# Second half's cross output projection and norms moved beside the first half's self-attention, second half's self-attention beside the shared expert

## What is computed

```python
# x (8, 100, 512), ctx (8, 361, 256); all float32
x = x + tanh(g_xattn) * xattn(layernorm(x), ctx, Wq, Wk, Wv, Wo)   # 16 heads of 128, 8 key-value heads
x = x + tanh(g_ffn) * ffn(layernorm(x), ...)

def ffn(x, ...):
    h = rms(x, w_ln1)
    q, k, v = h @ wq + bq, h @ wk + bk, h @ wv + bv      # 16 heads of 32
    q, k = rope(q, k)
    ctx = softmax(causal(q k^T / sqrt(32))) @ v
    x = x + ctx @ wo
    h = rms(x, w_ln2)
    probs = softmax(h @ w_router); combine = top 2 of 8 experts
    routed = sum over experts of combine * (silu(h @ w_gate_e) * (h @ w_up_e)) @ w_down_e      # width 352
    sh = (silu(h @ w_sh_gate) * (h @ w_sh_up)) @ w_sh_down * sigmoid(h @ w_sh_eg)              # width 1408
    return x + routed + sh
```

## Time and profile before

| | us |
|---|---|
| median of 3 runs (lowest, highest) | 997.44 (992.25, 1000.63) |
| the profiled execution's own time | 1002.25 |
| its span | 1000.4 |
| busy in the span: TensorE, VectorE, ScalarE, GpSimd | 903.5, 656.2, 565.2, 401.1 |
| mean granted TensorE clock | 0.952 |

### The profile page before, as it was taken

The page is one execution under the profiler, slowest core; times in us unless marked ns, Lnnn a source line. Parts: engine busy times, 40 slices in busy tenths (PEclk is TensorE's granted clock), DMA queues, the critical chain, the costliest instruction groups (busy, mean ns, idle before and its releaser), DMA issues.

```text
span 1000.4 us, 16144 instructions
## 1 busy us (share of the span) xinstructions
PE 903.5 (90%) x5713; PEld 834.9 (83%) x5713; DVE 656.2 (66%) x1492; ACT 565.2 (57%) x1433; POOL 401.1 (40%) x373
## 2 busy tenths in 40 slices
PE   4999999999999999997869787798888989999894
PEld 4889999999989999997848565597888988988894
DVE  4557777743747776722787757586745867888853
ACT  3656666644556666733436657554335767777750
POOL 3432322345532322345645321055371546555531
PEclk9999999999999999998977888799898989999998
DMA  5762000035510000044321111033577799999975
GB/s 140 218 226 84 1 1 1 11 105 146 164 57 16 2 1 1 12 92 118 95 82 44 43 54 33 12 97 104 173 211 213 229 280 271 298 295 288 285 181 144
DMA packets 125689, 120.76 MB, mean 121 GB/s; under 512 B 12645, under 2 KB 96557, under 8 KB 125009
## 3 DMA queue, kind: packets, MB, share of 16 engines
q1 hardware_dynamic: 106510, 96.09, 31.6%
q0 software_dynamic: 5120, 10.22, 5.1%
q10 hardware_dynamic: 13978, 13.41, 4.8%
HBM read 102.16 MB, written 17.53 MB: 120 GB/s over the span
## 4 chain that ended last, share of the span: by engine, by line
PE 54%; DVE 15%; DMA 15%; ACT 6%; issue 5%; POOL 3%; SPq 0%; ACTq 0%; POOLq 0%; DVEq 0%
PE bank L1978 49%; DMA eraw<-in_L_ffn_w_down_e_dram 5%; PE bank L2105 3%; DVE we L1301 3%; DMA s_sum<-yo,target 2%; DMA eraw<-in_L_ffn_w_up_e_dram 2%; ACT we L871 2%; ACT PF L1078 1%; DMA s_rows<-HR,idx 1%; DMA raw<-in_L_ffn_wq_dram 1%; POOL wf L1839 1%; DVE PQ L1485 1%; DMA raw<-in_L_ffn_w_sh_up_dram 1%; DVE sm L1508 1%; DMA sums<-s_sum 1%
## 5 line engine op out<-in xcount | busy, mean ns | idle before, releaser
L1868 POOL TENSOR_SCALAR SC<-SC,mx,anyv 100x361 f32<-100x361 f32 x128 | 81.4, 647 | 210.9 <-DVE mx L1414 200.9
L1839 POOL TENSOR_TENSOR wf<-raw,wf 128x512 fp32r<-128x512 f32 x54 | 74.2, 1382 | 142.9 <-ACT wf L857 142.9
L1851 POOL TENSOR_TENSOR we<-eraw,we 128x704 fp32r<-128x704 f32 x40 | 74.2, 1854 | 108.1 <-ACT we L871 106.6
L1839 POOL TENSOR_TENSOR wx<-raw,wx 128x512 fp32r<-128x512 f32 x64 | 83.1, 1305 | 79.3 <-ACT wx L857 79.2
L871 ACT ACTIVATE we<-eraw 128x704 fp32r<-128x704 f32 (+2 forms) x140 | 96.1, 719 | 32.6 <-DMA eraw<-in_L_ffn_w_down_e_dram 18.2
L1301 DVE TENSOR_TENSOR we<-eraw,we 128x704 fp32r<-128x704 f32 (+2 forms) x100 | 94.9, 967 | 29.2 <-ACT we L871 28.9
L1978 PE MATMUL bank<-H2h,wf 128*128 128x400 f32 x352 | 100.6, 353 | 0.0
L986 ACT ACTIVATE SC<-SC,mx 100x361 f32<-100x361 f32 x128 | 75.4, 593 | 27.9 <-DVE mx L1410 27.2
L857 ACT ACTIVATE wf<-raw 128x512 fp32r<-128x512 f32 x100 | 61.5, 627 | 27.6 <-DMA raw<-in_L_ffn_w_sh_down_dram 9.2
L1978 PE MATMUL bank<-QOh,wx 128*128 128x400 f32 x256 | 72.3, 355 | 5.0 <-POOL wx L1839 5.0
L1978 PE MATMUL bank<-XTh,wx 128*128 128x400 f32 x256 | 72.1, 354 | 3.2 <-POOL wx L1839 1.9
(11 more groups left out here) (265 smaller groups left out, 2790.1 us busy)
## 6 DMA issues: line engine op xcount, KB each, us to landing
eraw<-in_L_ffn_w_gate_e_dram SPq DMA_DIRECT2D x40, 352.0 KB
eraw<-in_L_ffn_w_up_e_dram SPq DMA_DIRECT2D x40, 352.0 KB
eraw<-in_L_ffn_w_down_e_dram SPq DMA_DIRECT2D x40, 256.0 KB
raw<-in_L_xattn_Wq_dram SPq DMA_DIRECT2D x32, 256.0 KB
raw<-in_L_xattn_Wo_dram SPq DMA_DIRECT2D x32, 256.0 KB
raw<-in_L_ffn_w_sh_gate_dram SPq DMA_DIRECT2D x22, 256.0 KB
raw<-in_L_ffn_w_sh_up_dram SPq DMA_DIRECT2D x22, 256.0 KB
s_rows<-Z SPq DMA_DIRECT2D x6, 800.0 KB
```

What stands on the lines that cost most here:

```text
L1839: eng.tensor_tensor(w[:, 1, :, :], raw[plan.raw[stream, u] % 4][:, :, :], f32(w[:, 0, :, :]), ALU.subtract).then_inc(sem("pool_w"), 1)
L1851: eng.tensor_tensor(w[0:rows, 1, 0:n], eraw[u % 6][0:rows, 0:n], f32(w[0:rows, 0, 0:n]), ALU.subtract).then_inc(sem("pool_e"), 1)
L1868: eng.tensor_scalar(sc, sc, m[:, 3, h:h + 1], anyv[:, b:b + 1], ALU.mult, ALU.mult).then_inc(sem("pool_p"), 1)
```

## The change

The list of steps after the second half's cross attention is written anew; the work itself is the same.

- The second half's `wo` units run tile by tile (f outermost) instead of u outermost, so tiles 0 and 1 are done after six of the twelve. Six units stand before `qk` of half 0, two beside it, and four beside the first four steps of half 0's self-attention. Half 1's `resid`/`norm1`/`square`/`row`/`turn` go beside steps 5 to 15 of it, and so do half 0's values; `qk` of half 1 begins at step 15.
- Self-attention is cut in two runs of 16 rounds (20 steps each). The epilogue of half 0 and half 1's values stand between them, after `po` of half 0. The second run has one gate or up group of half 0's shared expert beside each of its steps 1 to 19.
- `eroot` takes one square root per sequence instead of one per half, and each `er` is followed by the norm of the sequence before.
- Half 1's epilogue has 11 groups of the shared expert beside it; between `rank` and the first `xt` are 4 + 8 + 4 = 16; beside the 20 routed blocks are 11, the last of which has three units; three groups of three units come last.
- Six of half 0's `qk` units get their rest from VectorE instead of GpSimd. The map of SBUF and the use of PSUM banks are new: banks 0 and 1 stay free for the dense work beside self-attention, `CXh`/`CXl` are shared by the halves, and `bvb`/`ln2b` are loaded earlier.

The core of the diff:

```diff
+WO_ORDER = [[(u, f) for u in range(4) for f in range(KD)],
+            [(0, f) for f in range(KD)] + [(u, f) for f in range(KD) for u in range(1, 4)]]
+TILE_BANKS = (5, 6, 2, 3)
+SCORE_BANKS = (2, 3, 5, 6)
...
-    return [[("fetch_x",), ("wo", half, u, f)] for u in range(1, 4) for f in range(KD)]
+    return [[("fetch_x",), ("wo", half, u, f)] for u, f in WO_ORDER[half][KD:]]
...
 def epilogue_groups(h):
-    return ([[("er", h, i)] for i in range(HB)] + [[("eroot", h), ("erms", h, 0), ("erms", h, 1)]]
-            + [([("erms", h, i + 2)] if i + 2 < HB else []) + [("eh", h, i)] for i in range(HB)]
-            + [[("elog", h)], [("esoft", h)], [("etop1", h)], [("etop2", h)]])
+    out = []
+    for i in range(HB + 2):
+        out.append(([("er", h, i), ("eroot", h, i)] if i < HB else []) + ([("erms", h, i - 1)] if 1 <= i <= HB else [])
+                   + ([("eh", h, i - 2)] if i >= 2 else []))
+    return out + [[("elog", h)], [("esoft", h)], [("etop1", h)], [("etop2", h)]]
...
-def steps_routed(s1):
+def steps_routed(s1, beside):
...
-        yield from take(s1, 1)
+        if i * beside // NB < (i + 1) * beside // NB:
+            yield from take(s1, 1)
...
     yield from take(wo, 1)
-    for _ in range(AHEAD["f"]):
-        yield fetch
     yield ("row", 0)
     for i in range(HB):
-        yield from take(wo, 3)
+        yield from take(wo, 1)
+        yield fetch
         yield ("turn", i)
         if i + 1 < HB:
             yield ("row", i + 1)
-    yield from take(wo)
-    yield ("ffn_constants",)
-    dense = [g for n in range(8) for g in ([fetch, ("qk", 0, n)], [("rope", 0, n)])]
-    dense += [[fetch, ("vrow", k)] for k in range(KD)]
-    res = [[("resid", 4)], [("norm1", 4)], [("square", 4), ("row", 4), ("resid", 5)], [("norm1", 5)],
-           [("square", 5), ("row", 5), ("resid", 6), ("turn", 4)], [("norm1", 6)],
-           [("square", 6), ("row", 6), ("resid", 7), ("turn", 5)], [("norm1", 7)],
-           [("square", 7), ("row", 7)], [("turn", 6)], [("turn", 7)]]
-    yield from take(dense, 1)
-    for n in range(2 * HB + 2):
-        yield from take(dense, 1 if n == 8 else 2)
-        yield from take(res, 1)
-    yield from take(res)
-    yield ("router_split",)
-    yield from take(dense)
-    at = [[("at", n)] for n in range(8 * HB + 4)]
-    qk = [g for n in range(8) for g in ([fetch, ("qk", 1, n)], [("rope", 1, n)])]
-    yield from take(at, 1)
-    yield from take(qk, 1)
-    for n in range(12):
-        yield from take(at, 1)
-        yield from take(qk, 2 if n < 3 else 1)
-    yield from take(qk)
-    v = [[("vbat", 0), fetch], [("vadd", 0), ("vbat", 1), fetch], [("vadd", 1), ("vbat", 2)], [("vadd", 2), ("vbat", 3)],
-         [("vadd", 3), fetch, fetch]]
-    for _ in range(5):
-        yield from take(at, 1)
-        yield from take(v, 1)
-    yield from take(at, 2)
-    po = [[fetch, ("po", 0, m)] for m in range(KD)]
+    yield ("bias",)
+    yield from take(wo, 1)
+    for n in range(8):
+        yield from (fetch, ("qk", 0, n))
+        if n:
+            yield ("rope", 0, n - 1)
+        if n in (5, 7):
+            yield from take(wo, 1)
+    yield ("rope", 0, 7)
+    beside = {0: take(wo, 1), 1: take(wo, 1), 2: take(wo, 1), 3: take(wo, 1), 4: [("vbat", 0, 0), fetch],
+              5: [("vadd", 0, 0), ("resid", 4)], 6: [("vbat", 0, 1), fetch, ("norm1", 4), ("ffn_constants",)],
+              7: [("vadd", 0, 1), ("resid", 5), ("square", 4)], 8: [("vbat", 0, 2), ("row", 4), ("norm1", 5)],
+              9: [("vadd", 0, 2), ("turn", 4), ("resid", 6), ("square", 5)], 10: [("vbat", 0, 3), ("row", 5), ("norm1", 6)],
+              11: [("vadd", 0, 3), fetch, fetch, ("turn", 5), ("resid", 7), ("square", 6)], 12: [("row", 6), ("norm1", 7)],
+              13: [("turn", 6), ("square", 7)], 14: [("row", 7)], 15: [("turn", 7), fetch, ("qk", 1, 0)],
+              16: [fetch, ("qk", 1, 1), ("rope", 1, 0)], 17: [fetch, ("qk", 1, 2), ("rope", 1, 1)],
+              18: [fetch, ("qk", 1, 3), ("rope", 1, 2)], 19: [fetch, ("qk", 1, 4), ("rope", 1, 3), ("router_split",)]}
+    for n in range(4 * HB + 4):
+        yield ("at", 0, n)
+        yield from beside[n]
+    for n in range(5, 8):
+        yield from (fetch, ("qk", 1, n), ("rope", 1, n - 1))
+    for m in range(KD):
+        yield from (fetch, ("po", 0, m))
+        if m == 0:
+            yield ("rope", 1, 7)
     ep = epilogue_groups(0)
-    for _ in range(4):
-        yield from take(po, 1)
-        yield from take(at, 1)
-    for _ in range(9):
+    for i in range(HB):
         yield from take(ep, 1)
-        yield from take(at, 1)
-    yield ("moe0",)
-    s0 = up_groups(0, 0)
-    po = [[fetch, ("po", 1, m)] for m in range(KD)]
+        yield ("vbat", 1, i)
+        if i < 2:
+            yield fetch
+        if i:
+            yield from [("vadd", 1, n) for n in ((0, 1) if i == 1 else (i,))]
+    yield from (fetch, fetch)
     yield from take(ep, 1)
-    yield from take(s0, 1)
-    yield from take(at)
+    yield ("at", 1, 0)
     yield from take(ep, 1)
-    yield from take(s0)
-    yield from take(ep, 1)
-    yield from take(po, 2)
-    yield from take(ep, 1)
-    yield from take(po)
+    s0 = [g for j in range(NJ) for g in up_groups(j, 0)]
+    for n in range(1, 4 * HB + 4):
+        yield ("at", 1, n)
+        yield from take(s0, 1)
+        yield from take(ep, 1)
+    for m in range(KD):
+        yield from (fetch, ("po", 1, m))
     yield ("moe1",)
-    s0 = [g for j in range(1, NJ) for g in up_groups(j, 0, j == 1)]
+    s0 += down_groups(0)
+    s1, down = [g for j in range(NJ) for g in up_groups(j, 1)], down_groups(1)
+    s1 += [take(down, 3) for _ in range(KD)]
     ep = epilogue_groups(1)
-    for _ in range(9):
-        yield from take(ep, 1)
-        yield from take(s0, 1)
-    s0 += down_groups(0)
-    for n in (2, 1, 1, 1):
+    for n in (1, 1, 1, 1, 1, 1, 2, 1, 1, 1):
         yield from take(ep, 1)
         yield from take(s0, n)
     yield ("rank",)
-    yield from take(s0, 4)
+    yield from take(s0)
     for _ in range(AHEAD["e"]):
         yield ("fetch_e",)
     for b in range(B):
         yield ("rows", b)
-        yield from take(s0, 1)
-    yield from take(s0)
-    s1 = [g for j in range(NJ) for g in up_groups(j, 1)] + down_groups(1)
+        yield from take(s1, 1)
     yield from take(s1, 4)
     yield ("xload", 0)
     yield ("xload", 1)
     yield ("xt", 0)
     yield ("xload", 2)
-    yield from steps_routed(s1)
+    yield from steps_routed(s1, 11)
     yield ("sums",)
-    yield from take(s1, len(s1) - 3)
+    yield from take(s1, len(s1) - 1)
     for b in range(B):
         yield ("final", b)
     yield from take(s1)
...
-        on_dve = range(n_f - 46, n_f)
+        on_dve = [0, 1, 2, 3, 5, 7, *range(n_f - 46, n_f)]
...
+    CXh[0] = CXh[1] = held("CXh", 62784, [128, KD, HT], R)
+    CXl[0] = CXl[1] = held("CXl", 88384, [128, KD, HT], R)
...
+    def turned_bank(u):
+        return banks[4 if u % 2 else 7]
+    def norm_bank(what, b):
+        if b >= HB:
+            return banks[plan.bank[what, b]]
+        return banks[(6 if what == "resid" else 4) + b % 2]
...
-        def eroot(h):
-            b0 = h * HB
-            act.wait_ge(sem("dve_ms2"), b0 + HB)
-            eng.activation(rz[:, b0:b0 + HB], ms[:, b0:b0 + HB], ACT.Sqrt, bias=eps2[:, 0:1]).then_inc(sem("act_rz2"), 1)
+        def eroot(h, i):
+            b = h * HB + i
+            act.wait_ge(sem("dve_ms2"), b + 1)
+            eng.activation(rz[:, b:b + 1], ms[:, b:b + 1], ACT.Sqrt, bias=eps2[:, 0:1]).then_inc(sem("act_rz2"), 1)
...
             if h:
                 act.wait_ge(sem("pe_d"), 12)
+            else:
+                act.wait_ge(sem("pe_qk"), 16)
+                act.wait_ge(sem("pe_fv"), B)
...
+            if at >= 12:
+                dve.wait_ge(sem("dma_st1"), 16 * B)
...
+                if u == 0:
+                    pe.wait_ge(sem("dve_o"), 2 * NS)
+                elif u == 1:
+                    pe.wait_ge(sem("dve_ht"), HB)
```

327 lines of the change are left out of this document (144 added, 183 removed).

## The result

| | before | after |
|---|---|---|
| median of 4 runs each (lowest, highest), us | 997.18 (992.25, 1000.63) | 1023.39 (1019.36, 1025.8) |
| span of the profiled execution, us | 1000.4 | 1020.2 |
| mean granted clock | 0.952 | 0.956 |

The ratio of the times is 1.0263, with a 95% interval from 1.0206 to 1.0319: the change makes the kernel slower by about 26 us. The prediction was 994 us, with a range up to 1014.

A forecast was written before the change was run, and what follows sets the result against it. The prediction took VectorE and ScalarE to set the pace in both self-attention runs and DMA in the routed blocks. Its terms summed to 996.8 us, 3.6 under the span of 1000.4, giving 994 us, range 974 to 1014.

The forecast's parts named there:

- to the first qk: From 438.9 us to half 0's first qk: seven units and four turns, 17 us, with the wait beside XR taken as 0.
- first run: Half 0's self-attention with half 1's norms, half 1's qk and four po: 94 us, ending at 577.
- epilogue of half 0: Between the self-attention runs: VectorE's 4.0 us a sequence and 3 to end, 19 us, with TensorE's values hidden.
- second run: Self-attention beside 19 groups: TensorE needs 59 us, but VectorE's maximum waits behind gate operations, so 67 us.
- epilogue of half 1: After the second self-attention run, beside 11 groups: VectorE's chain, the router's logits and the choice show, 38 us.
- rank to the first block: From rank to the first routed block: scatters, ranks and first expert weights set the time, not TensorE; 53 us.
- routed blocks and tail: The end of the kernel: DMA bounds the blocks, 189.5 us with fewer shared units beside them; the tail keeps 44.4.
- eight steps with roots: Steps 6 to 13 of the first self-attention run, with two table loads each: 40 us.
- fall into waits: Sign of being wrong: the table loads of the first self-attention run cost little and its eight steps take under 4 us.
- TensorE's pace: Rival: TensorE sets the pace in the second self-attention run, the eight steps and the routed blocks; 978 us, chance 0.37.
- ScalarE's queue: Rival: ScalarE's queue bounds self-attention, from about 4 us a step in the second run, eight steps over 5.5; 1013 us, chance 0.20.
- The switches: Rival: each of 16 ScalarE function switches costs at most another load, 20.5 us in all; 1014 us, chance 0.05.

The follow-up runs named there:

- e12: The changed kernel with the load of XR issued beside half 0's first qk instead of at the head of the stage: 1020.4 us.
- e1: The changed kernel with the eight square roots of half 1's first norm replaced by a copy needing no table load, so results differ from the reference: 1013.4 us.
- e3: The changed kernel with six PSUM banks instead of two in half 0's epilogue with half 1's values: 1011.9 us.
- run 67: Not a follow-up run: the words give the 67 us predicted for the second self-attention run, which took 73.6 us.
- e13: The changed kernel with VectorE's share of each group placed behind its share of the next step, in the second self-attention run only: 1016.5 us.
- e7: The changed kernel with the 19 shared-expert groups of the second self-attention run moved behind it, ahead of half 1's output projection: 1039.6 us.

## Why the prediction was wrong, point by point

Measured against the prediction's own terms, in us of the profiled execution:

| term | predicted | measured | difference |
|---|---|---|---|
| to the first qk | 17 (456) | 22.4 (461.35) | +5.4 |
| qk with rope, to the first scores | 27 | 28.6 | +1.6 |
| first run | 94 | 103.6 | +9.6 |
| epilogue of half 0 | 19 | 24.3 | +5.3 |
| second run | 67 | 73.6 | +6.6 |
| po of half 1 | 9 | 9.5 | +0.5 |
| epilogue of half 1 | 38 | 35.7 | -2.3 |
| rank to the first block | 53 | 51.9 | -1.1 |
| routed blocks and tail | 233.9 | 231.6 | -2.3 |
| sum | 996.8 | 1020.1 | +23.3 |

**What was right.** The late stages: that six of the moved groups had been nearly free behind `rank`, that DMA sets the blocks' pace, that the late gain is small. Of "15 us or more" of idle TensorE between `rank` and `xt` there are 15.1, 8.6 of them a wait for the tokens. In half 1's epilogue, which was given 38 us and took 35.7, TensorE was busy for 31.7 us, not 28; the sum there was off, as three units less than 36.9 are 30.3. The eight steps with roots were given 40 us and took 41.9, with two loads each. The rule of the Trainium skill, page "ScalarE: Activation LUTs", section "What ACT_TABLE_LOAD costs", would have made them some 22 us longer; this trace, in which the load at 530.13 starts 0.01 us after the copy before it has ended, and the root 0.01 us after the load, disagrees again; before none of the 16 loads of this run is there a pause of more than 0.02 us.

**First qk.** The step that failed is "I take 0, as the units that were ready then suffice for the shorter list". The wait for weights beside `XR` did not go: ScalarE stood 3.0 us before a part of `wo`, and with it VectorE's row and TensorE's turn, 3.2 us; the half clock behind it, 0.59 over 4.2 us, is worth another 1.7 (an estimate from those two numbers). That is nearly all of the 5.4. And behind the wait, as e12 shows, stands a loop of 3.65 us a turn through ScalarE and VectorE, whose cover had gone from three units to one, so that even without the wait the first qk came 19.9 us after cross attention. The sum of TensorE's work was taken for the time.

**First run.** Rounds 0 to 5 took 21.7 us from the first scores, not 18, the eight `qk` 25.0, not 22, and the four `po` 10.4, not 9; the eight steps added 1.9. That the loads would "fall into waits" was what the prediction called its own refutation; e1 shows it more than half true: 20.5 us of loads cost 8.

**Epilogue of half 0.** The step that failed is "TensorE's values (11) are the cover, and hidden": it assumed that TensorE could run ahead. With two banks it cannot; with six (e3) the stretch took 18.1 us, under the 19 predicted. VectorE's price was right, and the bank ring was not read, though it stood in the change.

**Second run.** "In a step with a gate VectorE's maximum stands behind the gate's operations" named the mechanism, and TensorE's 59 us bounded the run from below. The term was mis-sized: two steps were given 6.7 us and the run 67, and it took 73.6. The 5.1 us between the changed kernel and e13 are what that queue costs; the prediction had 8 for the whole way from TensorE's 59 to 67. What it lacked is in the 59: e13's run takes 68.5, of which TensorE is busy for 62.7 at a granted clock of 0.95 and idle for 5.8. Part of that is the start, where TensorE waits 2.9 us for the last split and runs its first unit at half clock (a matmul takes 0.67 us in the row above).

**The rivals.** TensorE's pace (978, chance 0.37) needed TensorE full in both runs, and it was busy for 48.6 of 68.3 us and 65.2 of 73.6. (Its sum is off too: eight steps of 4.25 us are 6 under the 40, not 4.) ScalarE's queue (1013) came nearest to the time, but its two marks did not appear: 3.7 us a step in the second run, not over 4, and 5.2 in the eight steps, not over 5.5. Its own price for the second run, 3.8 a step, was nearer than the forecast's, but e13 shows VectorE's queue there. The switches did not cost double. What happened was none of them alone: six early terms were all too small, by 29 us together. Each was one engine's sum with a small allowance, in stretches where two or three engines in turn hold each other up.

## What to carry to other kernels

When work is moved to stand beside other work, look at both ends: what its old place then leaves bare (a chain of scatters, a loop of turns), and whether the queues and buffers of the new place let it run beside anything at all. In an engine that works in its program's order a step's late input holds up everything behind it, so sum the loop through all engines, not the fullest engine alone. And where several terms of a sum rest on "hidden", as here, their errors have one sign and add up: too fast.

## What the runs showed of the hardware

Some of VectorE's operations take up to two or three times as long beside some of GpSimd's. A row of 512 numbers without GpSimd, and one beside a subtraction of GpSimd, in the changed kernel (VectorE, then GpSimd):

```profile
447.93 0.75 DVE L1310 SCALAR_TENSOR_TENSOR HR<-Z,rz,ln1b 100x512 f32<-100x512 f32 x1
456.45 1.71 DVE L1310 SCALAR_TENSOR_TENSOR HR<-Z,rz,ln1b 100x512 f32<-100x512 f32 x1
```

```profile
456.33 1.28 POOL L1832 TENSOR_TENSOR wx<-raw,wx 128x512 fp32r<-128x512 f32 x1 [2.36 <-ACT wx L864]
```

GpSimd began first, at 456.33, and ended at 457.61; VectorE's operation ended 0.55 us later, so it seems to have stood still until then. Where VectorE began first it was GpSimd that took longer: a subtraction that began at 444.94, 0.12 us after such a row, took 2.38 us. The last additions of `rope` went as the first pair did, 1.3 to 1.7 us beside GpSimd and 0.58 in the last one, without it. Two things did not slow VectorE in this trace: an input in PSUM (17 splits into `QOl` in cross attention, 128x400, one input in PSUM, began beside a subtraction of GpSimd and took 0.57 us, as without one), and GpSimd's indirect transfers (five rows of 512 numbers beside the scatters took 0.74 us each). The Trainium skill has the rule, page "SBUF — State Buffer", section "SBUF: two separate sides": VectorE and GpSimd share a pair of ports as an exclusive lock, which concerns a VectorE operation with two inputs in SBUF only against a GpSimd operation that reads SBUF, and whichever starts first holds it for the whole instruction. These rows agree.

The granted clock follows how little TensorE has beside the self-attention: 0.51 over the bare run of e7 (34.6 us busy in 49.7), 0.91 over the changed kernel's run two, and 1.00 for the 25 us of e13 in which it never waits. That may be part of why eight of the 19 groups cost only 0.7 us each there; no run tested it.
